# Batch norm and two linear layers folded into the weighted sums of a graph network

## The reference, cut to what matters

```
m  = mean(x, axis=0);  v = var(x, axis=0)
h  = (x - m) / sqrt(v + 1e-5) * gamma + beta              # batch norm over the nodes
a_in  = segment_sum((h @ W_in  + b_in )[src] * iw[:, None], dst)
a_out = segment_sum((h @ W_out + b_out)[dst] * ow[:, None], src)
g  = concat(a_in, a_out) @ W_x2i + b_x2i + h @ W_h2h      # N x 2D
z, n = sigmoid(g[:, :D]), tanh(g[:, D:])
x  = layernorm(x + (1 - z) * n + z * h)
```

## Time and profile before

| what | value |
|---|---|
| median of 3 runs | 4138.27 us (4135.9 to 4142.09) |
| span of the profiled execution | 4129.6 us |
| PE busy | 3235.8 us (78%) |
| DVE busy | 2446.4 us (59%) |
| ACT busy | 1829.5 us (44%) |
| POOL busy | 1134.4 us (27%) |
| HBM read and written | 439.71 and 210.77 MB |

### The profile page before, as it was taken

One profiled execution on the slowest core, in us unless ns is written; L12 is line 12 of the kernel. 1 busy time (PEld: TensorE's weight loads), 2 busy tenths in 40 slices (PEclk: granted clock), 3 DMA queues, 4 the chain that ended last, 5 costly groups with the idle time before them and its releaser, 6 DMA issues. The chain is left out here.

```text
span 4129.6 us, 85621 instructions
## 1 busy us (share of the span) xinstructions
PE 3235.8 (78%) x18069; PEld 2388.7 (58%) x18070; DVE 2446.4 (59%) x6689; ACT 1829.5 (44%) x6323; POOL 1134.4 (27%) x908
## 2 busy tenths in 40 slices
PE   5666658998887859999543337989996899998988
PEld 4444437887876746767422226878885444544455
DVE  7999988888765643254688868777764200000554
ACT  1888882344455521021688748777772000000111
POOL 1788888888888401101000000000000000000002
PEclk9999999999999979999655559999998999999999
DMA  2444444678788846757565535444331443542047
GB/s 98 125 120 121 122 104 110 186 231 247 224 259 275 292 156 175 211 169 211 174 192 183 170 105 174 125 121 121 105 104 41 150 149 103 199 157 69 1 179 264
DMA packets 436836, 652.83 MB, mean 158 GB/s; under 512 B 101676, under 2 KB 293015, under 8 KB 436610
## 3 DMA queue, kind: packets, MB, share of 16 engines
q1 hardware_dynamic: 353154, 521.08, 40.7%
q10 hardware_dynamic: 53040, 121.95, 8.2%
q0 software_dynamic: 30544, 8.56, 3.0%
HBM read 439.71 MB, written 210.77 MB: 158 GB/s over the span
## 5 line engine op out<-in xcount | busy, mean ns | idle before, releaser
L1065 POOL DMA_INDIRECT slots<-all_B,put_index x800 | 1042.9, 1304 | 343.2 <-issue 338.0
L1950 POOL MEMSET c_T<- 128x28 f32 x1 | 0.1, 148 | 1983.5 <-POOLq L142 1983.5
L1315 ACT ACTIVATE lm_raised<-lm_hot,srt_words 128x125 f32<-128x125 bf16 x1200 | 356.3, 385 | 83.9 <-DVE lm_top L1230 66.9
L2498 DVE TENSOR_TENSOR upd_pre<-upd_po,upd_bias 125x512 f32<-125x512 f32 x25 | 17.3, 691 | 621.7 <-PE upd_po L2429 621.7
L1349 PE MATMUL lm_ps<-lm_v,lm_node 125*128 x1220 | 170.5, 184 | 267.3 <-DVEq L1217 95.2
L2073 PE MATMUL att_ps<-att_right,att_left 128*125 128x125 f32 x2380 | 314.1, 285 | 70.7 <-ACT att_right L2094 57.7
L1036 PE MATMUL put_ps<-put_right_in,put_left_in 128*128 128x125 f32 x2210 | 319.8, 295 | 63.1 <-ACT put_left_in L893 62.8
L2073 PEld LDWEIGHTS att_ps<-att_right,att_left 128*125 128x125 f32 x2380 | 284.5, 190 | 96.3 <-issue 85.4
L1036 PEld LDWEIGHTS put_ps<-put_right_in,put_left_in 128*128 128x128 f32 x2210 | 281.8, 202 | 87.2 <-ACT put_left_in L893 73.2
L2147 DVE SCALAR_TENSOR_TENSOR att_power<-soft_negated,srt_words,att_far 128x125 f32 (+1 forms) x1190 | 321.0, 344 | 3.8 <-ACT att_right L2094 3.3
L1651 PE MATMUL c_po<-c_halves,c_T 125*125 125x512 f32 x1250 | 320.1, 405 | 0.0
(11 more groups left out here) (418 smaller groups left out, 5816.7 us busy)
## 6 DMA issues: line engine op xcount, KB each, us to landing
c_T<-counts SPq DMA_DIRECT2D x255, 312.5 KB, 3.3
pair<-put_T ACTq DMA_DIRECT2D x125, 625.0 KB
att_ring<-hot SPq DMA_DIRECT2D x480, 160.0 KB
gio_T<-pair SPq DMA_DIRECT2D x60, 1250.0 KB, 5.9
hot<-put_hot SPq DMA_DIRECT2D x448, 160.0 KB
all_A<-in_edge_attr_dram SPq DMA_DIRECT2D x100, 448.0 KB
lm_planes<-src_rows SPq DMA_DIRECT2D x123, 320.0 KB, 3.6
counts<-put_T ACTq DMA_DIRECT2D x125, 312.5 KB
```

The costliest lines, as they stand in the source:

```text
L1065: nc.gpsimd.indirect_dma_start(slots, bass.IndirectOffsetOnAxis(index[:, C * g + j:C * g + j + 1], 0), stage[:, C * g + j, :], None).then_ ...
L1315: ins = nc.scalar.activation(raised[:, j % 2, c * P:(c + 1) * P], hot[:, j, c * S:c * S + P], ACT.Copy, scale=logit[:, ds(G * g + c, 1)])
```

## The change: what it does

The batch norm is written as `h = c * s + beta` with the centred rows `c = x - m` and a scale `s` for each feature. `phase_batch_norm` and the `wio` product are gone as phases, and so is `cat`.

- During the attention layer, POOL adds each finished block of `X` into a 125 x 256 tile `total` (L2241 of the new text). The mean is one product with it.
- `phase_streams` centres `X` into `A`, and multiplies all 14 jobs with these centred rows. The variance comes from one reduced tile of squares. The scale is applied by ACT when a job's sum leaves PSUM (`activation` with `scale=scol`).
- Between pieces of the jobs 1 and 2, PE multiplies `W_in` and `W_out` with the halves of `W_x2i` (`turn`, `fuse`), which gives gate weights `w` that take the scaled sums directly.
- The biases become, for each node, (sum of its tile's weights) times a fixed row. The row sums were stored with the tiles (`pair[:, o, ONE, :]`); PE makes the two fixed rows `u` (`bias`, `widen`) and the sums by node (`tally`). In `phase_gates` POOL makes each block's bias from them, up to four blocks ahead, and DVE waits for it (`laid`).
- The batch-normed rows are made by DVE in `B` during the streams. `gio_T` has 5 buffers in place of 8. The weights are loaded by POOL's and ACT's queues during the streams.

The diff, cut to its core:

```diff
 # phase_attended
-        return {"pool": lambda pool: None, "rows": rows, "act": act, ...}
+        def pool(pool):
+            total, totalled = k["total"][:, :], s.sem("totalled")
+            nc.gpsimd.memset(total, 0.0).then_inc(totalled, 1)
+            for d in range(NB):
+                pool.wait_ge(finished, d + 1)
+                pool.wait_ge(totalled, d + 1)
+                nc.gpsimd.tensor_tensor(total, total, X[:, d, :], ALU.add).then_inc(totalled, 1)
+            pool.wait_ge(totalled, NB + 1)
 # phase_streams: before, each of 14 jobs is 5 pieces of 10 products, and nothing else
-        HELD = 8
+        HELD = 5
+            @block.gpsimd    # POOL: wdir, wx, rows5 (10 DMAs), w[4:6], wc, base
+                pool.dma_start(wx, a["L2_gnn_W_x2i"]...).then_inc(weights_in, 16)
...
+                def variance():
+                    pe.wait_ge(squared, 1)
+                    t_.matmul(pm[0:P, D:2 * D], k["ones"][0:P, :], squares[:, :], ...).then_inc(varied, 1)
+                    for h in range(KC):
+                        ins = t_.matmul(pu[:, h:h + 1], squares[:, 128 * h:128 * h + 128], k["ones"][0:P, 0:1], ...)
...
+                t_.matmul(pm[0:P, 0:D], k["ones"][0:P, :], k["total"][:, :], ...).then_inc(meaned, 1)
+                for q in range(PIECES):
+                    if q == PIECES - 1:
+                        variance()
+                    stream(0, q)      # waits centred, q + 1
+                stream(1, 0)
+                pe.wait_ge(weights_in, 48)
+                turn(0)
+                pe.wait_ge(cols_in, 16 * 6)
+                pe.wait_ge(shifted, 1)
+                for o in range(2):
+                    bias(o)
+                stream(1, 1)
+                fuse(0, 0)
...
+                pe.wait_ge(fused_out, 4)
+                widen(0)
+                stream(2, 1)
+                widen(1)
+                stream(2, 2)
+                tally()
...
             # ACT, as a job leaves PSUM
-                        nc.scalar.copy(out[...], po[...]).then_inc(moved, 1)
+                        nc.scalar.activation(out[...], po[...], ACT.Copy, scale=scol[:, h:h + 1]).then_inc(moved, 1)
             # DVE
+                for part in parts:
+                    v.tensor_tensor(A[:, part, 0:D], X[:, part, :], wide(mean), ALU.subtract).then_inc(centred, 1)
+                for f, part in enumerate(parts):
+                    dve.wait_ge(centred, f + 1)
+                    ins = v.tensor_tensor(B[:, part, :], A[:, part, 0:D], A[:, part, 0:D], ALU.mult)
+                chain(ins)
+                v.tensor_reduce(squares[:, :], B[:, :, :].rearrange("p b n -> p n b"), AX.X, ALU.add).then_inc(squared, 1)
...
+                for part in parts:
+                    chain(v.tensor_tensor(B[:, part, :], A[:, part, 0:D], wide(scale), ALU.mult))
+                    chain(v.tensor_tensor(B[:, part, :], B[:, part, :], wide(bt), ALU.add))
 # phase_gates
-            def _(sp):    # fetch of cat, w, bias, wc: all gone
+            @block.gpsimd
+            def _(pool):
+                for d in range(NB):
+                    h = d % BIASES                       # BIASES = 4
+                    if d >= BIASES:
+                        pool.wait_ge(biased, d - BIASES + 1)
+                    for o in range(2):
+                        g.tensor_scalar(part[:, h, :], t["u"][:, o, :], sums[:, o, d:d + 1], None, ALU.mult).then_inc(weighed, 1)
+                        pool.wait_ge(weighed, 2 * d + o + 1)
+                        g.tensor_tensor(bias[:, h, :], part[:, h, :], bias[:, h, :] if o else t["base"][:, :], ALU.add).then_inc(laid, 1)
...
-                pe.wait_ge(ready, 64)
+                    dve.wait_ge(laid, 2 * d + 2)
-                    v.tensor_tensor(pre[:, d % 2, :], po[0:P, d % 2, :], bias[:, :], ALU.add).then_inc(biased, 1)
+                    v.tensor_tensor(pre[:, d % 2, :], po[0:P, d % 2, :], bias[:, d % BIASES, :], ALU.add).then_inc(biased, 1)
```

More of the change, by code:

```diff
@@ L2237, in phase_attended, with phase_streams @@
+        return {"pool": pool, "rows": rows, "act": act, "dve": dve, "start": lambda dve: None}
     phase_weighted(nc, k, "att", True, H, D + 1, None, make, attention, scratch)
-def phase_streams(nc, k, tag, sums):
+def phase_streams(nc, k, X, A, B, a_in, a_out, t, a):
+    KC = D // 128
     ctx = ExitStack()
     with ctx:
-        s = Scope(nc, ctx, tag)
-        jobs = [(H, by_dst, out, range(d, min(d + SET, NB))) for H, by_dst, out in sums for d in range(0, NB, SET)]
+        s = Scope(nc, ctx, "gio")
+        jobs = [(by_dst, out, range(d, min(d + SET, NB))) for by_dst, out in ((True, a_in), (False, a_out)) for d in range(0, NB, SET)]
@@ L2272, in _ @@
             @block.tensor
             def _(pe):
-                for i, (H, by_dst, out, group) in enumerate(jobs):
-                    w = len(group) * P
-                    if i >= 2:
-                        pe.wait_ge(moved, 2 * (i - 1))
-                    for q in range(PIECES):
[L2279 to L2288, removed]
+                t_ = nc.tensor
@@ new lines, in stream @@
+                def stream(i, q):
+                    by_dst, out, group = jobs[i]
+                    n, w = PIECES * i + q, len(group) * P
+                    if i >= 2 and q == 0:
+                        pe.wait_ge(moved, 2 * (i - 1))
+                    pe.wait_ge(landed[n % HELD], 16 * (n // HELD) + 16)
+                    for b in range(PB * q, PB * q + PB):
+                        if i == 0 and b % PB == 0:
+                            pe.wait_ge(centred, q + 1)
+                        tiles = (piece(n, group, by_dst)[0:P, :, (b - PB * q) * P:(b - PB * q) * P + P] if by_dst else
+                                 piece(n, group, by_dst)[0:P, b - PB * q, :])
+                        for h in range(2):
+                            ins = t_.matmul(po[:, i % 2, h, 0:w], A[:, b, 128 * h:128 * h + 128], tiles,
+                                            start=(b == 0), stop=(b == NB - 1))
+                    ins.then_inc(used, 1)
@@ new lines, in _ @@
+                stream(1, 1)
+                fuse(0, 0)
+                stream(1, 2)
+                fuse(0, 1)
+                turn(1)
+                stream(1, 3)
+                fuse(1, 0)
+                stream(1, 4)
+                fuse(1, 1)
+                stream(2, 0)
+                pe.wait_ge(fused_out, 4)
[4 more added lines that the diff above has]
+                tally()
+                for q in range(3, PIECES):
+                    stream(2, q)
@@ new lines, in _ @@
+                nc.scalar.activation(rcol, scol, ACT.Sqrt).then_inc(rooted, 1)
+                act.wait_ge(scaled, 1)
+                move(0)
+                for o in range(2):
+                    act.wait_ge(turned, o + 1)
+                    nc.scalar.copy(wt[:, o, :, :].rearrange("p t n -> p (t n)"), pt[:, :]).then_inc(turned_out, 1)
+                    for it in range(KC):
+                        act.wait_ge(fused, 2 * o + it + 1)
+                        nc.scalar.copy(t["w"][:, KC * o + it, :], pw[:, :]).then_inc(fused_out, 1)
@@ L2307, in phase_attention @@
         phase_attended(nc, k, H, X, scratch, (logit, negated))
[L2310 to L2325, removed]
-            def _(sp):
[L2327 to L2372, removed]
```

199 lines of the change are left out of this document (155 added, 44 removed).

## The result

The changed kernel takes 4043.56 us (median of 4, 4040.89 to 4048.22), the kernel before 4137.76: a ratio of 0.9771, 95% interval 0.976 to 0.9783. The forecast was 4033 us; 4043.6 lies in the range of 4020 to 4056, but outside the forecast's own 4024 to 4041. The profiled execution's span fell from 4129.6 to 4041.4 us, 88.2 us.

A forecast was written before the change was run, and what follows sets the result against it. The prediction took PE to bound streams and gates, with 138 us to work on between phases. Its terms, -112.3 + 16.0 - 11.8 - 1 + 1.5 + 2 = -105.6 us, took 4138.3 to 4033 us, range 4020 to 4056.

The forecast's parts named there:

- Term 1: From attention to streams: sums, store and weight loads go, 123.3 us becomes 11.0, a gain of 112.3 us.
- rival B: Streams start late or stall on other queues' loads and fewer buffers: 12 us more, 4045 us; chance 0.12.
- Term 2: Inside the streams: the products added there cost PE 16.0 us.
- Term 3: From streams to gates: the loads go, the semaphore clearing grows; 14.6 us becomes 2.7, a gain of 11.8 us.
- Term 4: First gate block: PE idles less ahead of it; a gain of 1 us, between 0 and 3.9.
- Term 5: Attention layer: POOL's 25 adds are mostly absorbed and cost 1.5 us, bounds 0 and 20.
- Term 6: Gates: DVE waits for POOL's bias, four instructions per block, mostly hidden; costs 2 us, at most 11.
- Rival A: Gates: POOL and DVE can't run together, a block takes about 6.0 us, 4045 us in all; chance 0.25.
- Rival C: Gates: POOL's bias sets the pace at 12.4 us per block, slower than before, 4202 us; chance 0.03.

The follow-up runs named there:

- all mends: The changed kernel with POOL's products as two-input instructions and POOL's and ACT's stream loads delayed until the first piece is used: 4027.7 us, ratio 0.9729.

## Why the prediction was right or wrong

- **Term 1** was right. The 1 us for shared DMA engines was 2.1; the two late-load kernels show it, so rival B's mechanism is real, but worth 2 to 4 us and not 12. Its other half, fewer buffers, costs nothing.
- **Term 2** was right: without the two delays of the loads the streams take 544.0 us against 528.4, 15.6 us for 16.0 forecast. The added products themselves take 14.9 us in the changed kernel's timeline. The narrow products ran at the low price of 0.11 us (1.84 us for 16 and the like). The reduction of the squares took 11.1 us where 7.5 was worked out, but it ended at 3175.6, and PE asked for it at 3194.2.
- **Term 3** was right to 0.1 us; twenty more clearings took 1.5 us, 0.07 us each, close to the 0.076 worked out.
- **Term 4** gave nothing in the profiled execution, but in the other kernels with the same PE program 6.3 to 9.1 us stood in the place of 9.3. The first four gate products, as the trace counts, took 3.78 us in the changed kernel at a granted clock of 0.50, 2.98 in the kernel with all mends at 0.63, and 1.98 at 1.00 in the one with POOL's two-input products: the gain is 0.1 to 3.0 us, by how soon the clock rises. PE's pause ahead of them is 3.3 us in all three, so why it rises sooner in some isn't shown.
- **Term 5** was put too high: 0.2 us, and none of it POOL's adds, since the layer takes as long without them.
- **Term 6 is the step that failed.** "I take 0.83 and 1.2 with gaps of 0.15: 4.7 us, hidden, and 2 us for what leaks." The two-input adds measured 1.27 us, the one-input products 1.57, not 0.83. The price came from an instruction of another kind (`affine_select`, 1.38 ns for a column over a fixed 0.12 us), and the assumption that one input is cheaper than two was false for these forms on POOL. With 1.57 the prediction's own formula gives 2 x 1.57 + 2 x 1.27 + 0.3 = 6.0 us, 16 us less 5 of lead, 11 us, near the measured 11.5. (That agreement is in part luck: the block came out at 5.97 us and the lead at 3.3.) The mechanism was named, and so was its sign: DVE waits for POOL's tile while POOL never pauses, 142.5 us busy of the 149 from 3705.4 to 3854.5. The upper bound of 6.0 us had the right size too, but from other parts (0.83, 1.53 and gaps of 0.32). What was off is the size of a product.
- **Rival A** had the right time, 4045, for a wrong cause. The clash is there, but it costs PE 0.06 us per block, since DVE, not POOL, does nearly all the waiting and has the slack for it. **Rival C** needed 9.8 us per block; the real one was 6.0.

## What to carry to other kernels

Before work is given to an idle engine, its rate for that very form of instruction has to be known: a form that looks cheaper can be dearer, and an engine that is "free" becomes the bound as soon as its block takes longer than the block of the engine it feeds. When a time agrees with a rival, look whether the cause does; here a kernel that drops the wait and keeps the work, and the rows of POOL working with nobody beside it, told the two apart. Of a fused phase, ask which part pays: the sum given to POOL during attention gave 1.8 us in the traces and nothing in the times, since the load of the first piece and the clock's rise had to be paid anyway.

## What the runs showed of the hardware

- POOL on 125 x 512 fp32: `tensor_scalar` 1.57 us with a scalar from SBUF, 1.49 with a constant; `tensor_tensor` 1.27 us, and 1.03 with one input broadcast. These are times with no DVE update beside them; beside updates the last two become 1.33 and 1.21 us (medians of the kernel with POOL's two-input products).
- The clash between POOL and DVE isn't even. Changed kernel, POOL and then DVE at the same time:

```profile
3772.83 1.27 POOL L2548 TENSOR_TENSOR upd_bias<-upd_part,sum_base 125x512 f32<-125x512 f32 x1
3774.20 1.61 POOL L2544 TENSOR_SCALAR upd_part<-sum_u,sum_sums 125x512 f32<-125x512 f32 x1
```

```profile
3772.39 0.43 DVE L2643 SCALAR_TENSOR_TENSOR upd_r<-upd_gate,upd_r 125x256 f32<-125x256 f32 x1
3772.85 1.53 DVE L2644 SCALAR_TENSOR_TENSOR upd_r<-upd_r,upd_gate 125x256 f32<-125x256 f32 x1
3774.41 0.80 DVE L2646 TENSOR_TENSOR all_X<-upd_r,all_X 125x256 f32<-125x256 f32 x1
```

The DVE instruction that began 0.02 us after POOL's two-input add ended 0.28 us after it, 1.53 us in place of 0.42; the one inside POOL's one-input product took 0.80, and POOL's product 0.04 us more than alone. In this kernel DVE waited much and POOL hardly; in the one with two-input products POOL was held up too, by the 0.18 us of a product given above. The Trainium skill, SBUF — State Buffer, section "Who interferes with whom", says that the later of the two is blocked until the first ends. The first pair agrees; the second doesn't, as DVE's 0.80 us end at 3775.21, inside POOL's product, which ends at 3775.81. Another product of the same kernel, from 3732.41 to 3734.02, has two DVE updates within it, one of 0.80 us and behind it, at 3733.46, one of 0.42. The measurement decides: the rule holds here against POOL's `tensor_tensor`, not against its `tensor_scalar`.
